# A message-passing layer on one core: loads moved to ScalarE, later node rounds, regions used twice, an earlier branch, and another order of the edge pairs

## The reference, cut to what matters

```
h   = relu(layernorm(x))                      # x: 3125 nodes x 64
msg = concat(h[dst], edge_attr)               # 53125 edges x (64 + 64)
m   = relu(msg @ W1a.T + b1a)                 # 53125 x 128
m   = m @ W1b.T + b1b                         # 53125 x 64
agg = segment_sum(m, src) / max(count, 1)     # 3125 x 64
z   = relu(concat(h, agg) @ W2a.T + b2a) @ W2b.T + b2b
out = x + concat(z, h) @ Wr.T + br
```

## Time and profile before

| | us |
|---|---|
| median of 3 runs (528.05 to 528.76) | 528.64 |
| profiled execution, its own time | 527.18 |
| span of the profile, first to last instruction | 525.4 |
| PE busy, 2889 matmuls | 410.0 |
| POOL busy, 404 instructions | 348.6 |
| DVE busy | 338.0 |
| ACT busy | 234.7 |
| mean granted TensorE clock, share of full speed | 0.905 |

### The profile page before, as it was taken

The page is one execution under the profiler, slowest core; times in us unless marked ns, Lnnn a source line. Parts: engine busy times, 40 slices in busy tenths (PEclk is TensorE's granted clock), DMA queues, the critical chain, the costliest instruction groups (busy, mean ns, idle before and its releaser), DMA issues.

```text
span 525.4 us, 8550 instructions
## 1 busy us (share of the span) xinstructions
PE 410.0 (78%) x2889; PEld 364.1 (69%) x2889; DVE 338.0 (64%) x786; ACT 234.7 (45%) x540; POOL 348.6 (66%) x404
## 2 busy tenths in 40 slices
PE   5644655999789898687789888997887889986791
PEld 4434545875678787676678778897776878985681
DVE  7778364455485876738376776877635766767781
ACT  3331815441565266476716346373463354400370
POOL 4777777766277777777777777776772777777000
PEclk9776977795879999888999999999789999999996
DMA  7996998522499599776879689699249999787511
GB/s 187 317 326 159 261 255 272 163 94 75 146 307 297 206 333 275 211 247 208 317 230 307 209 249 366 227 343 276 102 146 372 293 339 308 242 272 215 138 44 43
DMA packets 66077, 123.19 MB, mean 234 GB/s; under 512 B 8793, under 2 KB 35726, under 8 KB 66030
## 3 DMA queue, kind: packets, MB, share of 16 engines
q1 hardware_dynamic: 53518, 90.80, 57.4%
q0 software_dynamic: 12512, 31.80, 17.9%
HBM read 67.86 MB, written 54.70 MB: 233 GB/s over the span
## 4 chain that ended last, share of the span: by engine, by line
PE 36%; DVE 23%; POOL 13%; issue 9%; DMA 8%; ACT 5%; SPq 4%; DVEq 0%; ACTq 0%; POOLq 0%
POOL slots_dram L632 12%; PE bank L1392 8%; PE bank L1374 7%; PE bank L1402 7%; DMA dstb<-in_dst 5%; PE bank L1356 5%; DVE perm L810 5%; DVE oh L859 3%; PE bank L1327 2%; PE bank L1427 2%; DVE sums L885 2%; DVE x_hi L798 2%; DVE x_lo L800 2%; PE bank L1424 1%; DMA rows<-slots_dram 1%
## 5 line engine op out<-in xcount | busy, mean ns | idle before, releaser
L632 POOL DMA_INDIRECT slots_dram<-pay,pos_i x271 | 265.2, 978 | 99.0 <-issue 80.2
L1392 PE MATMUL bank<-rows,oh 128*125 128x130 f32 x1150 | 141.0, 279 | 26.3 <-DVE oh L859 25.9
L1392 PEld LDWEIGHTS bank<-rows,oh 128*125 128x125 f32 x1150 | 133.1, 190 | 33.7 <-issue 32.5
L859 DVE TENSOR_TENSOR oh<-bank,rows 128x1500 f32<-128x1500 f32 (+5 forms) x72 | 85.7, 1194 | 33.1 <-DMA rows<-slots_dram 20.0
L618 POOL DMA_INDIRECT pairs_dram<-pay,pos_c x80 | 76.9, 962 | 37.2 <-issue 21.6
L1131 ACT ACTIVATE pay<-bank 128x512 f32<-128x512 f32 x68 | 39.5, 594 | 95.8 <-PE bank L1356 95.6
L1356 PE MATMUL bank<-pw,eo 128*128 128x128 f32 x542 | 73.4, 292 | 3.8 <-ACT pay L1131 2.6
L1356 PEld LDWEIGHTS bank<-pw,eo 128*128 128x128 f32 x542 | 69.2, 206 | 5.0 <-ACT pay L1131 3.0
L1144 ACT ACTIVATE eo<-dstb,minus_lane 64x512 f32<-64x512 int32 x56 | 39.8, 711 | 72.1 <-DMA dstb<-in_dst 54.9
L1402 PE MATMUL bank<-perm,x_hi 116*128 116x256 f32 (+1 forms) x160 | 42.3, 354 | 25.3 <-DVE perm L810 25.2
L1374 PE MATMUL bank<-pwx,moved 128*128 128x131 f32 x320 | 47.2, 306 | 10.3 <-ACT pw L1120 7.8
(11 more groups left out here) (215 smaller groups left out, 485.9 us busy)
## 6 DMA issues: line engine op xcount, KB each, us to landing
rows<-slots_dram SPq DMA_DIRECT2D x16, 864.0 KB, 7.9
rows<-pairs_dram SPq DMA_DIRECT2D x16, 864.0 KB, 11.6
dstb<-in_dst SPq DMA_DIRECT2D x34, 256.0 KB, 9.1
eo<-in_edges_T SPq DMA_DIRECT2D x34, 256.0 KB, 8.6
slots_dram<-zeros SPq DMA_DIRECT2D x9, 756.0 KB, 10.5
pairs_dram<-zeros SPq DMA_DIRECT2D x6, 864.0 KB, 18.9
rows<-slots_dram SPq DMA_DIRECT2D x8, 648.0 KB, 9.5
xs<-in_edges_rows SPq DMA_DIRECT2D x20, 232.0 KB
```

Of the source, the lines that this page charges most:

```text
L632: pool.indirect_dma_start(out=slots_dram[:, :], out_offset=bass.IndirectOffsetOnAxis(ap=pos_i[:, u, k:k + 1], axis=0), in_=pay[:, u, k, :] ...
L859: V.tensor_tensor(oh2[:, r % 2, 0:n, :], marks_near.unsqueeze(1).to_broadcast((128, n, BN)), rows[:, sum_no[r] % RR, 0:n, MARK:ONE].to_bro ...
L1392: last = T.matmul(o[0:BN, v * SW:(v + 1) * SW], oh2[:, r % 2, n, :], rows[:, sum_no[r] % RR, n, 0:SW], start=(t == 0), stop=(t == TB[ph] - ...
```

## The change

- ORDER becomes OOOO, three times CO, twice CCO, three times CO, and OOOOO. There are 10 paired and 17 old pairs as before. The paired groups are now 8, 9, 12, 13, 16, 17, 20 to 23, 26 to 29, 32, 33, 36, 37, 40 and 41, and groups 42 to 53 are old.
- The phases 2 to 5 of the old pairs get no regions of their own. Their rows are written over the regions of phase 0 (phase 2) and of phase 1 (phases 3, 4 and 5), whose rows have been read back by then; GpSimd waits for those reads. They aren't cleared. Their marks are raised by 128, and the one-hot of such a round subtracts it, so that what is left of the earlier phase matches nothing.
- The node rounds are ready from group 14 on and only behind old groups.
- For the old groups from the seventh on ScalarE issues the load of the edge features itself, ahead of the one-hot, and from the eleventh on the load of the destinations, behind the one-hot of the fourth old group before. SP issues neither.
- The edges of both groups of a paired pair are loaded, cast and turned into features one group (two for the load) before the pair, not each before its own group. Where two paired pairs follow each other, this comes at the end of the second group of the first.
- Every engine waits for `bd`, not for `flag`, and branches; SP waits for the output's landing behind the branch.

```
-ORDER = "OOOO" + "CO" * 10 + "OOO"
+ORDER = "OOOO" + "CO" * 3 + "CCO" * 2 + "CO" * 3 + "OOOOO"
...
+    OVER = [None, None, 0, 1, 1, 1]
+    FRESH = [ph for ph in range(NPH) if OVER[ph] is None]
...
+    TAG = [0 if ph in FRESH else 128 for ph in range(NPH)]
...
+    NODES_FROM = 14
...
-        return kind != "sum" or g >= END_GROUP[ph] + AFTER_PHASE[ph]
+        if kind != "sum":
+            return g >= NODES_FROM and g in O_GROUPS
+        return g >= END_GROUP[ph] + AFTER_PHASE[ph]
...
+        def paired_next(g):
+            return [C_GROUPS.index(g + v) for v in (1, 2)] if g % 2 and g + 1 in C_GROUPS else []
...
             for g in range(3, LG):
-                if g >= 6 and g in C_GROUPS:
-                    load_paired_edges(C_GROUPS.index(g))
-                elif g >= 6:
+                if g >= 6 and g in O_GROUPS and n < ACT_FROM + DB:
                     load_dst(n)
-                    load_edges(n)
                     n += 1
-                for ph in range(1, NPH):
+                for ph in FRESH[1:]:
...
+                for c in paired_next(g if g in C_GROUPS else g + 1):
+                    load_paired_edges(c)
...
-            sp.wait_ge(S["out"], 16 * sum(len(parts) for parts in OUT_PARTS))
-            sp.wait_ge(S["flag"], 1)
+            sp.wait_ge(S["bd"], 1)
             is_bad = sp.value_load(flag[0:1, 0:1], min_val=0, max_val=1)
...
+            sp.wait_ge(S["out"], 16 * sum(len(parts) for parts in OUT_PARTS))
...
-                    pool.wait_ge(s_fill[STARTS.index(n // 2)], 16 * len(CLEAR_PIECES))
+                    ph = STARTS.index(n // 2)
+                    if ph in FRESH:
+                        pool.wait_ge(s_fill[ph], 16 * len(CLEAR_PIECES))
+                    else:
+                        for r in range(RR):
+                            pool.wait_ge(s_rows[r], loads_of(OVER[ph], r))
...
-            pool.wait_ge(S["flag"], 1)
+            pool.wait_ge(S["bd"], 1)
...
-                if half == 0:
-                    features(c)
...
+                if ph < NPH and TAG[ph]:
+                    V.scalar_tensor_tensor(oh2[:, r % 2, 0:n, :], seen, -float(TAG[ph]), near, ALU.add, ALU.is_equal).then_inc(S["oh2"], 1)
...
             def rounds_after(g):
+                ahead = paired_next(g)
+                ranked = any(rounds[r][0] == "crank" for r in after[g])
                 for r in after[g]:
                     if rounds[r][0] == "ccount" and r >= 1:
                         take(r - 1)
                     hots(r)
+                    if ahead and not ranked and g not in C_GROUPS:
+                        features(ahead.pop(0))
                     if r >= 1:
                         take(r - 1)
                 if after[g] and rounds[after[g][-1]][0] in ("ccount", "crank"):
                     take(after[g][-1])
+                for c in ahead:
+                    features(c)
...
             def onehot(n):
                 g = O_GROUPS[n]
+                act.wait_ge(S["H"], made(O_GROUPS[n - EB]))
+                act.dma_start(eo[rest_half(n), n % EB, :], edges_T[:, g * GE:(g + 1) * GE]).then_inc(s_ea_in[n % EB], 16)
                 act.wait_ge(s_dst[n % DB], 16 * (n // DB + 1))
-                act.wait_ge(S["H"], made(O_GROUPS[n - EB]))
...
+                if n + DB < len(O_GROUPS):
+                    g = O_GROUPS[n + DB]
+                    act.dma_start(dstb[p, n % DB // 2, :], dst[g * GE:(g + 1) * GE].rearrange("(o e) -> o e", o=1).to_broadcast((WS, GE))
+                                  ).then_inc(s_dst[n % DB], 16)
...
-                    if g + 1 in C_GROUPS:
-                        round_features(c + 1)
...
                     for u in range(UNITS):
                         relu_unit(c, u)
+                    for c in paired_next(g):
+                        round_features(c)
...
-            pe.wait_ge(S["flag"], 1)
+            pe.wait_ge(S["bd"], 1)
```

More of the change, by code:

```diff
@@ L90, in gnn_layer @@
     ROOM = [min(C[ph] * 128, 32 * math.ceil((C[ph] * 128 - expected(ph) + 4.5 * math.sqrt(expected(ph))) / 32)) for ph in range(NPH)]
-    LEAST = [C[ph] * 128 - ROOM[ph] for ph in range(NPH)]
-    assert all(0 < ROOM[ph] <= min(256, C[ph] * 128) for ph in range(NPH))
-    BEGIN = [sum(C[:ph]) * NB * 128 for ph in range(NPH)]
-    SLOTS = sum(C) * NB * 128
+    OVER = [None, None, 0, 1, 1, 1]
+    FRESH = [ph for ph in range(NPH) if OVER[ph] is None]
+    LEAST = [C[ph] * 128 - ROOM[ph] if ph in FRESH else 0 for ph in range(NPH)]
+    assert all(0 < ROOM[ph] <= min(256, C[ph] * 128) for ph in FRESH)
+    BEGIN, used = [], {}
+    for ph in range(NPH):
+        home = ph if ph in FRESH else OVER[ph]
+        first = sum(C[v] for v in FRESH if v < home)
+        BEGIN.append((first + used.get(home, 0)) * NB * 128)
+        if ph not in FRESH:
+            used[home] = used.get(home, 0) + C[ph]
+            assert used[home] <= C[home]
+    SLOTS = sum(C[ph] for ph in FRESH) * NB * 128
+    TAG = [0 if ph in FRESH else 128 for ph in range(NPH)]
     SPILL = 2 * GE * max(PAIRS)
@@ L354, in gnn_layer @@
         s_dst = [sem(f"dst_loaded_{u}") for u in range(DB)]
[L355 removed]
+        s_fill = {ph: sem(f"regions_cleared_{ph}") for ph in FRESH}
         s_sc = [sem(f"rows_scattered_{u}") for u in range(PB)]
@@ L372, in region, with loads_of @@
             return slots_dram[first:first + m * C[ph] * 128, :].rearrange("(v p t) w -> p v (t w)", p=128, t=C[ph])
+        def loads_of(ph, u):
+            return 16 * max([0] + [n // RR + 1 for n, r in round_of.items() if rounds[r][1] == ph and n % RR == u])
         def round_tiles(r):
@@ L696, in _, with phase_of @@
             link(V.scalar_tensor_tensor(srcq[:], srci[:], -float(NB), src_in[:], ALU.mult, ALU.add))
+            def phase_of(j):
+                return sum(j >= first for first in STARTS[1:])
             def ranks_a(j):
```

34 lines of the change are left out of this document (21 added, 13 removed).

## The result

The changed kernel takes 552.2 us in the median of its runs (548.4 to 553.8). The kernel before, run beside it, takes 528.7 us (528.1 to 533.3). The ratio of the runs is 1.041, with a 95% interval of 1.033 to 1.050: 23.5 us slower in the medians, where 3 were forecast. The profiled execution took 551.3 us, 24.1 us more than the one before, with a span of 549.6 us. Some executions of a kernel are a few per cent slower than others of the same kernel; the ratios in this document leave the slow ones out, but the profiles of the order alone and of the end alone are of slow executions.

The account below looks back on a forecast made before the run. GpSimd's fixed scatter work and the supply (TensorE, VectorE, ScalarE) were taken as two clocks bounding the kernel. Waits of 32.2 against 23.1 us add 9.1, the end saves 6.1: 528.6 + 3.0, about 531.6 us; 8-in-10 range 517 to 539.

Parts of the forecast that it names:

- the end: Behind the last scatter: GpSimd's drain starts sooner, near 497 us, and TensorE is last; a gain of 6.1 us.
- it could be there at 286.4 - 10.1 = 276.3 us: At group 33: without waits GpSimd could arrive 10.1 us sooner, as an old pair ahead becomes a paired one.
- the supply's pace: TensorE, VectorE and ScalarE up to group 33: 9.8 us more from steps, -4 spreading rounds, +2 crank rounds, +3 ScalarE's loads.
- the features in the new step: Groups 21 to 22 and 27 to 28: both groups' features stand uncovered, making the step 10.1 us, 6.7 if covered.
- I count 0 here, with up to 4 us of gain: The second paired group's features leave the path, but PE's waits for one-hots mostly stay: 0, up to 4 us gain.
- the rank rounds in paired groups: Two crank rounds in groups 20 and 26, read by VectorE ahead of the next one-hot: 2 us, range 0 to 4.
- They come back by group 33, since this work is only put off: Waits at 103 to 145 us vanish as node rounds leave groups 7 to 12, but return by group 33.
- ScalarE's loads, +3: ScalarE's load issues delay its copies in groups 21, 22, 27 and 28: 3 us taken, from nothing to twice 5 us.
- the 8.1 us at group 46 go away: Phase 2 rounds come from group 49 on and no longer hold up SP ahead of destinations, ending GpSimd's 8.1 us wait.
- The supply did not keep up: Rival: idle TensorE takes the rounds, half the features and ScalarE's issues are hidden; 22 us of waiting, 521.4 us; chance 0.36.
- ScalarE's issues were not dear: Rival: 3 us more per pair of issues on the path, steps at upper bounds; 40 us of waiting, 539 us; chance 0.10.
- the drain did not stay: Rival: GpSimd's 9.2 us drain depends on what it waits for, so the end keeps its length; 537.7 us; chance 0.07.

Follow-up runs that it names:

- the order alone: The kernel before with the new ORDER alone: 554.8 us, ratio 1.025.
- the end alone: The kernel before with the sooner branch alone, every engine waiting for `bd` and not `flag`: 528.5 us, ratio 0.991.
- the three repairs: The changed kernel with node rounds from group 7 on, each paired group's features made ahead of its own one-hot, and rank rounds one group sooner: 539.5 us, ratio 1.011.
- node rounds early: The changed kernel with node rounds given out from group 7 on again: 544.3 us, ratio 1.023.
- features as before: The changed kernel with each paired group's features made ahead of its own one-hot, loads and casts back in their old place: 544.0 us, ratio 1.013.
- rank rounds sooner: The changed kernel with rank rounds of pairs behind another paired pair in old groups 19 and 25, not paired groups 20 and 26: 557.4 us, ratio 1.055.
- one double pair: The changed kernel with two paired pairs in a row (CC in ORDER) once in place of twice: 538.0 us, ratio 1.012.
- the old order with loads by SP: The changed kernel with the old ORDER, node rounds from group 7 on, and old groups' loads issued by SP: 534.5 us, ratio 1.003.

## Why the prediction was right or wrong

**Right: what bounds the kernel.** Two clocks, GpSimd's fixed work and the supply. The 24.2 us come out of GpSimd's waits and the end alone, and the waits are for ScalarE's positions at the groups that the prediction named.

**Right: the end.** -6.1 us forecast; the stretch behind the last scatter is 6.3 us shorter, and 7.0 us in the run of the end alone.

**Right: "it could be there at 286.4 - 10.1 = 276.3 us".** GpSimd came to group 33 at 330.8 us with 55.1 us of waits behind it: 275.7 us without them.

**Wrong: the supply's pace.** The sum put the last activation of group 33 at 297.4 + 9.8 (steps) - 4 + 2 + 3 = 308.2 us. It came at 330.5, 22.3 us later. In the run with the three repairs (node rounds early, features as before, rank rounds sooner) it comes at 310.6. That this is near 308.2 is luck. With the step of 7.5 us that this run has in place of 10.1, and no rank round in a paired group, the prediction's terms give 297.4 + (139.1 + 15.0 - 149.5) - 4 + 3 = 301.0 us for it. So the three repairs give 19.9 us where the terms say 7.2, and 9.6 us more are missing in the order itself. Of these 8.4 are found: the rank rounds lengthen the steps ahead of 20 and 26 by 4.8 and 3.6 us from an old group as well, and the sum had no term for that. The 12 further tiles of sum rounds are 24 matmuls, by an estimate 2.8 us (24 of them took 2.82 us at 204 us in the changed kernel). The gain of 4 us from spreading rounds was not measured by itself.

**Wrong in size: the features in the new step, and "I count 0 here, with up to 4 us of gain".** The sum had 10.1 us in place of 6.7 for two steps, 6.8 us in all, and nothing else. Taken back alone, the new place brings the activation of group 33 from 330.5 to 319.5 us and the waits down by 12.6. The step is 12.5 us with it and 7.5 without. Of these 5.0 us the 2.4 above the forecast are TensorE's at a granted clock of 0.57, behind a stretch with 1 us of work in 6; no term stood for the clock. No gain came in this order.

**Wrong in size: the rank rounds in paired groups.** This is the term that was furthest off for its size: 2 us taken, 0 to 4 as bounds. Against the place one group sooner they cost 9.2 and 9.4 us behind group 13, in two kernels with the features as before, and the sooner place is not free either. Each puts 3.6 us of VectorE's work ahead of a one-hot, and two of them are 7 us, above my upper bound already. In the changed kernel itself their price was not isolated.

**Wrong: "They come back by group 33, since this work is only put off".** In the old order 12.8 us go away early and 15.5 come back by group 33; in the new one 12.0 and 17.6. The net, 5.6 us of waits in the new order and 5.4 to 5.9 in the old, goes with ratios that fall by 0.018 and 0.005 to 0.023, but the early part of it varies by as much between executions. With the features as before it is not seen (320.3 us against 319.5 at group 33, 46.1 us of waits against 42.5), so this term depends on the others.

**Not borne out: ScalarE's loads, +3.** In the changed kernel they save 2.6 us of waits, which is within what the runs can tell. In the old order with the features in the new place they save 17.3 us, and 18 us of time. With the features as before the waits are those of the kernel before, 23.1 us. "Most of them hold nothing up until the last groups" was right for the kernel before, and wrong for one whose features come ahead of the pair: at group 21, where one wait for destinations was followed, the copy that TensorE needs stood behind it. The issues were not dear: ScalarE pays 0.47 us in the median, where SP paid 0.66 and up to 4 (duration ns min, median, max):

```profile
L1189 ACTq DMA_DIRECT2D dstb<-in_dst x24: 472/472/478, 52.6 to 426.4; - x24
```

The rule of the Trainium skill (DMA: Bandwidth & Descriptors, Issuing engines are not separate DMA queues) speaks of the sequencer's time alone, and here what counted was in whose queue, and behind what, the issue stood.

**Partly right: "the 8.1 us at group 46 go away".** In the new order they do: ScalarE is done with the first half of group 46 13.8 us before GpSimd comes to it. In the old order a wait of 1.9 to 6.4 us comes at group 47: the rounds of phase 2 stand ahead of its hidden part on TensorE, and VectorE waits for their rows.

**The rivals.** The supply did not keep up, ScalarE's issues were not dear, and the drain did not stay. The rival that was missing is the sum of the small terms: the prediction closed by saying that they would decide.

## What to carry over

When a change moves work of a fixed length away from ahead of a point, the others have to be there sooner by that length; that arithmetic held to within 1 us here. What can't be priced at nothing is work that is moved from a place beside other work into a chain of engines waiting for each other: put the whole new chain together, and compare it with the chain that would be there without the move. A total that comes out near the forecast is no proof of its terms: give the run that you compare with its own sum. And a wait that an engine has for a transfer is to be judged by what stands behind it in that engine's queue, not by whether its own result is late.

## What the runs showed of the hardware

The spread of the kernel before lies in its early part. From 100 to 150 us TensorE was busy for 46.2 us in the execution that was profiled first, with a granted clock of 0.82. In the run with the end alone, the same program up to there, it was busy for as long with less work, at a clock of 0.64, between the levels of 1.2 and 2.4 GHz and nearer the lower:

```profile
100.00:150.00 50.00, 46.02 (x176) 35.02 (x176) 21.05 (x53) 17.93 (x42) 24.84 (x26) 0.64 0.33 100
```

176 matmul records stand there in place of 225, and GpSimd waited 20.8 us up to group 13 in place of 12.0. The kernels with late node rounds have 1.1 to 7.1 us of waits in that part. Whether this makes their times steadier is not settled. Ten runs of the kernel with one double pair, which has them late, lay within 6.1 us, and ten of the end alone, which has them early, within 12.2. But ten of the old order with loads by SP, early too, lay within 6.5. Why the clock is granted differently for the same program, these runs don't say.

GpSimd's drain took 8.15 to 9.23 us in all 18 profiles, whether it started 11 us behind the last scatter or 33. TensorE's compare and branch took 3.6 to 4.0 us in the five profiles where it was read, SP's 0.04 to 0.06 us.
